# A chain of graph layers on one core: node blocks dealt out to other passes, statistics a part ahead of the roots, and the last pass split in two

## The reference

```python
x = layernorm(x + L0(x))   # x + W2 softplus(W1 segment_sum(attr, dst))
x = layernorm(x + L1(x))   # (x Wself + mean_w(x[src]) Wneigh) / 2
x = layernorm(x + L2(x))   # relu(x ws + segment_sum((x wn)[src], dst))
x = layernorm(x + L3(x))   # two Chebyshev convolutions, K = 3, with a hidden width of 256
```

## Time and profile before

| what | us |
|---|---|
| median of 3 runs | 4258.1 (4257.22 to 4259.97) |
| the profiled execution | 4258.12 |
| its span, first to last instruction | 4256.3 |
| DVE busy in the span | 3308.1 (78%) |
| PE busy | 3198.7 (75%) |
| POOL busy | 2589.6 (61%) |
| ACT busy | 2513.5 (59%) |

### The profile page before, as it was taken

The page is one execution under the profiler, slowest core; times in us unless marked ns, Lnnn a source line. Parts: engine busy times, 40 slices in busy tenths (PEclk is TensorE's granted clock), DMA queues, the critical chain, the costliest instruction groups (busy, mean ns, idle before and its releaser), DMA issues.

```text
span 4256.3 us, 74138 instructions
## 1 busy us (share of the span) xinstructions
PE 3198.7 (75%) x20676; PEld 2496.8 (59%) x20676; DVE 3308.1 (78%) x13225; ACT 2513.5 (59%) x7409; POOL 2589.6 (61%) x2650
## 2 busy tenths in 40 slices
PE   5699777768888888777788789998888899911111
PEld 2366466656666666666677766666666699911111
DVE  8889889978888888899999975555555588755554
ACT  0067689967777777677744457776666566511111
POOL 6667688856556656566376645544444356477777
PEclk9999999989999999999999999999999999955555
DMA  0066445642222222344344445554656466633332
GB/s 23 26 174 188 145 167 210 214 154 61 66 63 64 66 64 63 91 146 132 121 143 138 144 133 191 207 194 161 200 198 203 159 213 213 194 119 96 97 96 73
DMA packets 312017, 575.80 MB, mean 135 GB/s; under 512 B 69646, under 2 KB 98119, under 8 KB 311610
## 3 DMA queue, kind: packets, MB, share of 16 engines
q1 hardware_dynamic: 235322, 443.56, 30.8%
q0 software_dynamic: 76288, 127.51, 10.9%
HBM read 301.23 MB, written 271.14 MB: 134 GB/s over the span
## 4 chain that ended last, share of the span: by engine, by line
DVE 32%; PE 24%; POOL 16%; issue 14%; ACT 9%; DMA 3%; POOLq 0%; SPq 0%; DVEq 0%; ACTq 0%
DVE bn L1014 6%; POOL rows L599 6%; POOL out_dram L716 4%; PE ps L1779 4%; PE ps L1929 4%; DVE y L1119 3%; DVE mv L1019 3%; ACT outb L1501 3%; POOL node_put L587 3%; PE ps L1654 3%; PE ps L1857 2%; PE ps L1944 2%; PE ps L1945 2%; DMA state_h<-hb 2%; DVE u L1095 2%
## 5 line engine op out<-in xcount | busy, mean ns | idle before, releaser
L599 POOL DMA_INDIRECT rows<-state,rows_of_src x588 | 558.9, 951 | 435.2 <-PE ps L1893 223.6
L599 POOL DMA_INDIRECT rows<-lap,rows_of_lap x392 | 391.5, 999 | 318.5 <-PE ps L1893 153.5
L635 POOL TENSOR_TENSOR y<-xin,c0h 128x512 f32<-128x512 f32 x245 | 313.0, 1277 | 316.4 <-DVE bn L1014 252.4
L1654 PE MATMUL ps<-ident,y 128*128 128x128 f32 x1960 | 301.9, 282 | 217.6 <-DVE y L1119 142.4
L665 POOL DMA_INDIRECT looked<-node_table,look_idx x392 | 371.5, 948 | 108.6 <-issue 96.6
L1672 PE MATMUL ps<-ident,rows 128*128 128x128 f32 x392 | 102.4, 358 | 423.3 <-ACT rows L1327 409.8
L1654 PEld LDWEIGHTS ps<-ident,y 128*128 128x128 f32 x1960 | 227.4, 144 | 326.9 <-DVE y L1119 237.2
L1014 DVE BATCH_NORM_STATS2 bn<-y 128x6 f32<-128x128 f32 x1764 | 378.8, 277 | 28.0 <-POOL y L635 27.8
L1876 PE MATMUL ps<-V,hT 128*128 128x128 f32 x3136 | 386.0, 277 | 2.6 <-ACT hT L1492 2.5
L1857 PE MATMUL ps<-yTc,G02c 128*128 128x512 f32 x784 | 376.5, 603 | 0.0
L1876 PEld LDWEIGHTS ps<-V,hT 128*128 128x128 f32 x3136 | 368.5, 193 | 4.8 <-ACT hT L1492 4.6
(11 more groups left out here) (287 smaller groups left out, 9538.4 us busy)
## 6 DMA issues: line engine op xcount, KB each, us to landing
state_h<-hb SPq DMA_DIRECT2D x98, 512.0 KB, 4.0
xin<-in_x_dram SPq DMA_DIRECT2D x196, 256.0 KB, 3.4
out_dram<-outb SPq DMA_DIRECT2D x196, 256.0 KB
xe<-state SPq DMA_DIRECT2D x147, 256.0 KB
state<-outb SPq DMA_DIRECT2D x98, 256.0 KB
state<-oe SPq DMA_DIRECT2D x98, 256.0 KB
h_pre<-hb SPq DMA_DIRECT2D x49, 512.0 KB, 4.3
rows<-in_edge_attr_10x_dram SPq DMA_DIRECT2D x48, 320.0 KB
```

The source lines that it names most:

```text
L599: gp.indirect_dma_start(out=dest[:, at, k, 0:width], out_offset=None, in_=table_, in_offset=bass.IndirectOffsetOnAxis(ap=index[:, c:c + 1] ...
L635: gp.tensor_tensor(y0[:, g.b], xin[:, g.r if p == "nodes" else g.b], all4(c0h[:, :]), ALU.add)\
L1654: i = t.transpose(bank(bk)[:, k, :], source[:, k, :], ident[:, :])
```

## The change

Up to the pass `nodes` every engine's instructions stay as they are. From there on:

- **Parts.** The pass `nodes` keeps 81 instead of 98 blocks' worth of parts. The merged passes get 66, 70, 44, 38 and 48 (`L1` to `LH`), and a new merged pass `LA` gets 70. The pipeline is one part-turn longer: 603 parts.
- **Order in a part.** `node_part` is written anew for DVE, ACT and PE. The statistics of a block's input stand one turn earlier (block gn = g+1), and between the statistics of a tile and the root, and between the root and its reciprocal, other work of the part stands. The store to `out` and ACT's `outb` move to another part.
- **Last pass.** `LU` becomes `LA` (gathers, scan, norm, store to a scratch tensor `last_out`; with node parts) and `LB` (49 loads of `last_out` and the 196 scatters, nothing else). The sum of the third state and its bias, which `LU` made, is made in `T2` on DVE (`near` there was a copy by ACT).
- **L1.** The bias is added by PE (a product with a row of ones) and ACT copies the product out of PSUM; DVE did both before. **L2.** The last norm goes from DVE to ACT, which needs an offset from DVE.
- **Looks.** 322 of the 392 stand in `nodes`, 35 each in `L1` and `L2`; the weights are made at the end of `L2`.
- **T2 on SP.** The stores of a quad stand ahead of the loads of a later one.

```diff
-ALONE = BLOCKS // 2
+ALONE = 81
-NODE_PARTS = PARTS * (BLOCKS + 4)
-MERGED = ("L1", "L2", "T1", "T2", "LH")
-SHARE = {"L1": 57, "L2": 57, "T1": 57, "T2": 57, "LH": 58}
+NODE_PARTS = PARTS * (BLOCKS + 5)
+MERGED = ("L1", "L2", "T1", "T2", "LH", "LA")
+TAIL = {"L1": 4, "L2": 4, "T1": 2, "T2": 3, "LH": 2, "LA": 4}
+SHARE = {"L1": 66, "L2": 70, "T1": 44, "T2": 38, "LH": 48, "LA": 70}
+LOOKS_ALONE = 322
...
@@ sync: T2's stores first
+                    if p == "T2" and g3.inside(QUADS):
+                        h_kept.wait(sp, p, g3)
+                        sp.dma_start(quad_of(state_h, g3), hb[:, g3.b]).then_inc(more_st.of(g3), 16)
+                        oe_store(g3, near_kept)
                     state_load(g.less(-early))
...
@@ gpsimd: the last pass
-                if part != 1 and g.c < ALONE:
-                    look(2 * g.c + part // 2)
+                look(dealt(LOOKS_ALONE, q, PARTS * ALONE))
...
+            merged_pass("LA", lap2, rows_of_lap)
+            enter(pool, "LB")
+            for c in range(QUADS):
+                g = Turn(c)
+                rows_out_in.wait(pool, "LB", g)
                 for k in range(4):
                     gp.indirect_dma_start(out=out, in_=oe[:, g.r, k, :], in_offset=None, bounds_check=NODES - 1,
...
@@ vector: node_part, in the order after the change
                 if part == 0:
+                        sd0.wait(dve, p, g)
+                        v.reciprocal(rs[:, 0, g.b, :], sd[:, 0, g.b, :]).then_inc(rs0.sem, 1)
...
+                        stats(2, y3[:, g3.b], bn3)
...
                         v.scalar_tensor_tensor(u2[:, g1.b], bank(4), 0.0, y1[:, g1.b], ALU.max, ALU.add)\
...
-                            i = v.scalar_tensor_tensor(y1[:, g.b, k, :], bank(4 if shared else 3)[:, k, :], dev(0, g.b, k),
+                            i = v.scalar_tensor_tensor(y1[:, g.b, k, :], bank(6 if shared else 3)[:, k, :], dev(0, g.b, k),
...
@@ vector: L1, L2 and T2
-                        v.tensor_tensor(y3m[:, :, :], bank(LEFT), all4(b1c[:, :]), ALU.add).then_inc(step.sem, 1)
+                        own_kept.wait(dve, p, g)
...
-                    for k in range(4):
-                        i = v.tensor_scalar(oe[:, g.r, k, :], y1m[:, g.r, k, :], mvm[:, g.r, k, 0:1], rsm[:, g.r, k:k + 1],
-                                            ALU.subtract, ALU.mult)
+                    v.scalar_tensor_tensor(offm[:, g.r, :], mvm[:, g.r, :, 0], -1.0, rsm[:, g.r, :], ALU.mult, ALU.mult)\
...
+                        v.tensor_tensor(xe[:, g1.r], xe[:, g1.r], all4(gb2_row[:, :]), ALU.add).then_inc(state_biased.sem, 1)
...
+                        v.tensor_tensor(oe[:, g2.r], bank(TURNED), xe[:, g2.r], ALU.add).then_inc(near_kept.sem, 1)
...
@@ scalar: node_part
                 if part == 2:
+                        root(p, g3, sd3, mv3, sd[:, 3, g3.b, :], mv[:, 2, g3.b, :, 1], EPS1)
+                        root(p, g1, sd2, tv2, sd[:, 2, g1.b, :], tmpv[:, g1.b, :], EPS2)
                         keep(p, g, y1T_kept, y1_turned, [(p2_made, 1)], yTb[:, :, :], 0 if shared else 1)
+                        squares(p, g)
+                        root(p, gn, sd0, mv0, sd[:, 0, gn.b, :], mv[:, 0, gn.b, :, 1], EPS4)
...
@@ scalar: L1 and L2
-                        oe_st.wait(act, p, g2, back=RING)
-                        a.activation(oe[:, g2.r], bank(TURNED), ACT.Copy).then_inc(near_kept.sem, 1)
+                    if p == "L1" and g1.inside(QUADS):
+                        keep(p, g1, own_kept, product, [(step, 1)], y3m[:, :, :], LEFT)
+                    if p in ("L1", "L2", "LA") and g3.inside(QUADS):
                         scaled(g3)
...
@@ tensor: L1
+                        t.matmul(ps[:, LEFT, :], ones[0:1, :], all4(b1c[:, :])[0:1], start=True, stop=False)
```

More of the change, by code:

```diff
@@ L1190, in carry @@
                     summed.wait(dve, p, g)
-                    (first_product if p in ("T1", "T2") else product).wait(dve, p, g, back=2)
+                    (turned if p == "LA" else first_product if p in ("T1", "T2") else product).wait(dve, p, g, back=2)
                     if p == "T1":
@@ L1423, in _, with softplus_of @@
-            edge_pass("tgt0")
+            def softplus_of(g):
+                p, log, lin, made = "tgt0", hTs[g.b][:, 0], hTs[g.b][:, 1], bank(FIRST[g.b])
+                first_product.wait(act, p, g)
+                product.wait(act, p, g, back=2)
+                a.activation(log, made, ACT.Abs, bias=b1_col[:, :]).then_inc(softplus.sem, 1)
+                a.activation(lin, made, ACT.Relu, bias=b1_col[:, :]).then_inc(softplus.sem, 1)
+                softplus.wait(act, p, g, k=1)
+                a.activation(log, log, ACT.Exp, scale=-1.0).then_inc(softplus.sem, 1)
+                softplus.wait(act, p, g, k=3)
+                a.activation(log, log, ACT.Ln, scale=0.5, bias=HALF).then_inc(softplus.sem, 1)
@@ L1425, in src0_turn, with tgt0_turn @@
+            def tgt0_turn(g):
+                for late, work in ((1, softplus_of), (3, tgt0_norm), (2, tgt0_root)):
+                    if g.less(late).inside(QUADS):
+                        work(g.less(late))
+            enter(act, "tgt0")
+            a.preload_act_table_set("natural_log_exp_and_others")
+            run_turns(QUADS, LATE["tgt0"], tgt0_turn)
+            leave(act)
             def src0_turn(g):
@@ L1775, in _, with tgt0_sums @@
-            edge_pass("tgt0")
+            def tgt0_sums(g):
+                p = "tgt0"
+                if not g.inside(QUADS):
+                    return
+                attr_in.wait(pe, p, g)
+                ew_put.wait(pe, p, g)
+                if g.c == QUADS - 1:
+                    pe.wait_ge(zeroed, 1)
+                    pe.wait_ge(tail_in, 16)
+                carried.wait(pe, p, g, back=2)
+                for k in range(4):
+                    t.transpose(bank(g.b)[:, k, :], rows[:, g.r, k, 0:P], ident[:, :])
+                    i = t.transpose(ps[0:33, 2 + g.b, k * P:(k + 1) * P], rows[:, g.r, k, P:ATTR + 1], ident[:, :])
+                i.then_inc(summed.sem, 1)
@@ new lines, in tgt0_second, with tgt0_turn @@
+            def tgt0_second(g):
+                p = "tgt0"
+                softplus.wait(pe, p, g)
+                step.wait(pe, p, g, back=1, k=1)
+                for k in range(4):
+                    for j in range(2):
+                        i = t.matmul(bank(6)[:, k, :], hTs[g.b][:, j, k, :], W2T[:, :], start=j == 0, stop=j == 1)
+                i.then_inc(product.sem, 1)
+            def tgt0_turn(g):
+                tgt0_sums(g.less(-1))
+                if g.inside(QUADS):
+                    tgt0_first(g)
+                if g.less(1).inside(QUADS):
+                    tgt0_second(g.less(1))
@@ L1923, in layer @@
                         i.then_inc(product.sem, 1)
+                    if p == "LA":
+                        step.wait(pe, p, g, back=1)
+                        turn4(p, g, turned, agg[:, g.b], TURNED)
                     if p == "T1":
```

761 lines of the change are left out of this document (249 added, 512 removed).

## The result

The changed kernel took 4038.6 us (median of 4 runs, 4037.6 to 4051.9), the kernel before 4259.0 beside it: a ratio of 0.949, interval 0.947 to 0.951. Forecast were 4033 us, with 3960 to 4120 as the range. The profiled execution has a span of 4036.2 us, 220.1 less than before.

A forecast was written before the change was run, and what follows sets the result against it. Barriers split the kernel into stages with different limits: neither DVE nor PE full in nodes, DVE in L1 and L2, PE in T1 and LH, GpSimd's queue last. Stage terms summed to -225 us: 4033 us, range 3960 to 4120.

The forecast's parts named there:

- L1: Merged pass L1: 382 us, 3 longer than before, with PE and DVE nearly full; bounds 365 and 400.
- T2: Merged pass T2: 416 us, 53 shorter, from fewer parts and SP's stores going first; bounds 395 and 440.
- LA: New merged pass with gathers, scan and 70 parts: 362 us, DVE at nine tenths; bounds 345 and 400.
- Node pass: Pass nodes: 628 us against 834.3, 206 shorter, with blocks of 7.65 us in place of 8.39.
- DVE alone would need 7.4: Node pass: without its two waits and with dependent pairs parted, DVE would need 7.4 us a block, against 8.39.
- the ring through ACT: Node pass: the chain from tmpv through ACT's roots, copy and squares would add a DVE wait of some 0.25 us a block.
- Rival A: Node pass: the new order gives nothing, blocks stay at 8.39 us, total 4092; chance 0.13.
- rival C: Merged passes: parts with nothing to hide them expose turning and copy, deciding from 0.63 us a part; slower; chance 0.06.
- L2: Merged pass L2: 356 us, 11 shorter, as the norm leaves DVE and 13 parts come; bounds 345 and 375.
- T1, LH: Merged passes T1 and LH: 13 and 10 parts fewer on PE at 2.39 us each, -31 and -24 us.
- Rival B: LA: PE stays at the low clock, so LA takes 471 us, total 4142; chance 0.05.
- LB: Last pass, 196 scatters back to back at 1.29 us each: 262 us; bounds 255 and 510.

The follow-up runs named there:

- e6: Changed kernel with GpSimd making y0 only after VectorE's x3, in the node pass alone: 3982.4 us, ratio 0.934.
- e8: As e6, but five VectorE instructions of a node part again stand right behind the one whose result they need: 4079.1 us, ratio 0.957.
- e1: Changed kernel with the old deal of parts (98 blocks alone, 57 parts in each of L1 to LH): 4075.3 us, ratio 0.957.
- e5: Changed kernel with at most one part in a turn and 89 blocks alone: 3951.1 us, ratio 0.927.
- e3: Changed kernel with L1's own products made and copied earlier, and SyncE's loads ahead of its stores again in T2: 4093.6 us, ratio 0.961.
- e9: Kernel before with T2's stores ahead of loads, L2's norm on ScalarE, and outb in part 0 in the node pass: 4176.0 us, ratio 0.981.
- e4: Changed kernel with L1's bias and L2's norm back on VectorE, and T2's near rows copied by ScalarE again: 4118.5 us, ratio 0.967.
- e2: Changed kernel with GpSimd making y0 only after VectorE's x3, in all passes with node parts: 4096.8 us, ratio 0.962.

## Why the prediction was right, step by step

That the sum came out 5 us off is luck: L1 was 31 us too low, T2 26 and LA 14 too high.

*Node pass* (628, came 632.5): right in size by luck, with two errors that cancel. "DVE alone would need 7.4" was 0.4 too high, since the pairs that the order parts are worth more: 6.99 us are reached (e6), and 0.13 a pair (e8). "A new wait of some 0.25 us" on the ring through ACT never came; in its place GpSimd's add held up `off3` by 0.78 us. At the same deal the pass fell from 834.3 to 762.9 (e1), with 70 looks and the weights gone from it; a block fell from 8.39 to 7.73, or 0.66 us, and my 8.39 - 7.65 was 0.74. Rival A is out.

*L1* (+3, came +33.9, past my upper bound of 400): the step that failed. I priced the nine parts at 22 us by busy time and let them fill what room there was. All nine became second parts of a turn and cost 59 us (e1, e5). The trace of the kernel before would have said 42 (nine times 4.7), had I read its turns. The edits of the pass and the new order, which I had at -19 (-30, +18, -7), gain 25 us at the old deal. That VectorE would wait for the copy y3m held (35.8 us in 31 times, I had 18), but taking the copy's chain apart gave 6 us (e3). So the mechanism of rival C, a part with nothing to hide it, was there; its place and its size were wrong. It was not every part by 0.63 us but each second part in a turn, by 6.

*L2* (-11, came -2): the norm's move was right (-47.4 in e9, I had -45), the 13 parts too (+31.6, I had +32). The rest of the change cost about 14 there at the old deal (319.6 in e9 to 333.4 in e1), where I had 2 (9 - 7); which of its edits did, the new order of a part, the looks or the weights, was not tried.

*T2* (-53, came -79.2, past my lower bound of 395): the 19 parts gave 34.2 (I had 45), SyncE's order 12.4 alone (20), and the sum on VectorE, which I priced as 12 us lost, gains 14 (e4). The remaining 19 us come with the new order of a part or from edits that need each other: undoing SyncE's order in the changed kernel costs 53 (e3). The edits don't add, and which of them lifts which is open.

*T1, LH*: -33.6 and -17.4 for -31 and -24. A part costs 2.0 and 1.7 us there, not 2.39; the reason is open. In T1 the 13 parts gave only 25.5, and 8.1 more came at the old deal (e1), where I had put nothing.

*LA* (362, came 348.0): VectorE nine tenths busy (313.7), as said, but half of its 34.3 idle us come with the second parts and not with the tail that I added (17.5 are left in e5); the clock 0.87, a little under the 0.9 I gave, and 0.50 in e1 where PE has only 96 of 261.5 us to do. Rival B is out: the parts themselves keep PE up. *LB* (262, came 265.0): scatters start every 1.29 us, 196 of them from 3775.0 to 4026.0, and land after 2.2. That a scatter doesn't wait for the landing of the last held.

## What to carry to other kernels

- A part of other work is free only while something stands beside it: price it by the turn it goes to, and look at turns with none, one and two of it apart. Mean busy times said that L1 had room; its turns said 6 us, and those of the kernel before 4.7.
- When waits vanish and a loop doesn't get as short as its instructions allow, compare the durations of the same instruction before and after: time in which another engine holds an instruction up can be booked as busy (`off3`, 0.93 us for 0.15).
- A wait added on a queue is paid for by all that stands behind it; what gained 60 us in one stage cost over 100 in others (e2).

## What the hardware showed that I had not expected

- A VectorE instruction of 4 numbers a lane with both inputs in SBUF took 0.93 us in place of 0.15 beside GpSimd's add, and ended with it.
- A VectorE instruction that needs its forerunner's result costs 0.13 us more than one that doesn't: 0.67 us for five in a block.
